# Attention logits of a four-layer graph network: products and gates kept in PSUM, a signed scalar product

## The chip, the cores and the metric

The kernel runs on one core of one Trainium2 chip. The metric is the device time of one execution in microseconds (us), from the first to the last instruction with what lies around them. All data are float32. The engines are TensorE (PE; its weight loads are shown as PEld), VectorE (DVE), ScalarE (ACT), GpSimd (POOL) and SyncE (SP, which only issues DMAs here).

## The reference, cut to what matters

The network has four message-passing layers over one graph of 3,125 nodes and 103,125 edges. The change touches only layer 1, a graph attention whose edge features are 64 scalars `s` and 32 vectors `v` of three components. For each edge, with `y0` and `y1` (three numbers) its spherical harmonics:

```python
def _cg_tp(s, v, y0, y1, w_ss, w_sv, w_vs, w_vv0, w_vv1):
    out_s = concatenate([w_ss * s * y0, w_vv0 * (einsum('eci,ei->ec', v, y1) / SQRT3)])
    out_v = concatenate([(w_sv * s)[:, :, None] * y1, w_vs[..., None] * v * y0,
                         w_vv1[..., None] * (cross(v, y1) / SQRT2)], axis=1)
    return out_s, out_v
msg_s = (s_n @ Ws_src)[src] + (s_n @ Ws_dst)[dst]        # and msg_v in the same way
w1 = rbf @ W_rbf                                         # 224 weights per edge
m1_s, m1_v = _cg_tp(msg_s, msg_v, y0, y1, *split(w1))
a = (m1_s @ W_alpha).reshape(e, H, AS_)
a = sum(where(a > 0, a, 0.2 * a) * alpha_dot, axis=-1)   # the logits
val_s, val_v = m1_s @ Ws_val, einsum('ecx,cd->edx', m1_v, Wv_val)
val_v = val_v * sigmoid(val_s @ Wg)[..., None]
val_s = sigmoid(val_s)
m2_s, m2_v = _cg_tp(val_s, val_v, y0, y1, w2_ss, w2_sv, w2_vs, w2_vv0, w2_vv1)
h = (m2_s @ Ws_vlin, einsum('ecx,cd->edx', m2_v, Wv_vlin))
```

## The kernel before, in words

`attention_logits` (L967) makes the logits and the rows `h` for all edges. The edges are taken in 202 groups of 512: each partition holds 4 edges (`TPG`), and most tiles have the shape 128 x 4 x something. Every engine runs its own program, a loop over groups `g` unrolled four times (`rounds`), and the engines meet by counting semaphores. `hold(eng, k, sem, value)` is one wait and one increment of an idle counter; the order of instructions on each engine is the order in which they are written.

In step `g` each engine does parts of several groups:

- DVE: `head(g+1)`, `mid(g)`, `tail(g-1)`. The head adds the two gathered rows (L1253) and makes the first tensor product in `feat`: scalars by weights (L1259, L1261), all nine products of the three components with the three harmonics in `vy` (`with_planes`, L1237), the scalar product as a reduce (L1263), the cross product as two subtractions (`cross`, L1242 and L1243), and three products with the weights (L1264, L1267, L1269). The mid takes what TensorE made of it: L1278, L1282 and L1287 make the gated vector `vec`, L1279 and L1289 the logits, then `with_planes` again (`ty`, L1237), a reduce (L1296) and `cross` into `z`. The tail (L1304, L1308) finishes the row that is stored. `HEAD`, `MID` and `TAIL` count the instructions of each part, for the waits.
- ACT, one queue in this order (L1093 to L1137): `take_feat` for pieces 0 and 1 of group g+1 (PSUM to SBUF, L1101), the copy of the scalars of `c2` for group g-1 into `hrow` (L1108, signals `hs_ready`), `take_feat` of piece 2, four copies of `vec` scaled by y0 (L1113), four copies of `wps` scaled by y0 into `wy` for group g+2 (L1121), three copies of the turned `z` (L1126), then for group g+1 the sigmoid for the gates, the relu, a copy and a sigmoid (L1129 to L1132), and four scaled copies (L1135).
- PE in step g (L1150 on): the second map of group g-1 into `c2` for rows 0 and 1, the turn (transpose) of `feat` piece 0 of group g+1, second map row 2, turn of piece 1, second map row 3 (this one signals `c2_ready`), turn of piece 2, the weights `wps` of group g+2 (L1189), and then the first map of g+1 (`scal`, `fv`) by rows with the turns of `z` of group g between them. All turns write the one bank `tps`, so each waits until ACT has taken the one before it. The turn of `feat` piece 0 waits for `head_ops`, the turn of `z` piece 0 for all of `mid(g)`, then for `sy_ready` and `vy_ready`.
- POOL issues eight gathers for a group four groups ahead of its head (L1085). SP loads the harmonics, the indices and the radial basis, and stores `hrow`.

PSUM is full: `wps`, `scal` and `c2` have two banks each, `fv` and `tps` one.

## Time and profile before

| | us |
|---|---|
| median of 3 runs (lowest, highest) | 6447.02 (6443.19, 6455.58) |
| the profiled execution: its time | 6445.45 |
| the profiled execution: its span | 6443.7 |
| first L1253 of the logits stage to its last L1108 | 1275.6 to 3695.8 |

Over the whole span PE is busy 75%, DVE 75%, ACT 36% and POOL 66%. In the logits stage the order is different, so the stage is read by itself: by a window over it, by its groups of instructions, and above all by the timeline of one group of edges. A row of a timeline has the start in us from the beginning of the span, the duration, the engine, the line, what it writes and reads, and in brackets how long the engine was idle before it and who released it. Where a helper holds the instruction, the line is that of the helper: both nine-fold products are L1237, both cross products L1242 and L1243, all turns L1144.

### The profile page before, as it was taken

How to read it: one execution, taken by the hardware profiler on the slowest of the kernel's cores; microseconds unless marked ns; L12 is line 12 of the kernel's file. 1: busy time of each engine (PE TensorE's matmuls, PEld its weight loads, DVE VectorE, ACT ScalarE, POOL GpSimd, SP SyncE). 2: the span in 40 equal slices, each digit the busy share in tenths (PEclk: the TensorE clock that was granted, in tenths of full speed). 3: DMA queues.
4: the chain of work that ended last, by engine and by line, in shares of the span. 5: the costliest groups of instructions: out<-in, count | busy, mean ns of one | idle time of the engine just before them, and what ended most of it. 6: DMA issues, size and time to landing. Idle time of an engine off the chain costs nothing. (4 is left out here: it accounts for less than half of the span.)

```text
span 6443.7 us, 162517 instructions
## 1 busy us (share of the span) xinstructions
PE 4855.9 (75%) x45499; PEld 3778.9 (59%) x45500; DVE 4808.7 (75%) x11056; ACT 2316.4 (36%) x6999; POOL 4230.3 (66%) x4250
## 2 busy tenths in 40 slices
PE   6666667488888888888888769877766677777775
PEld 3444445377777777777777757644444464444445
DVE  5777776489989899898998764477777756666665
ACT  1100002266666666666666567400100021000001
POOL 5777775177767777777777347277777727777772
PEclk8888888699999999999999979888888887777777
DMA  3333332133333333333333247222222212222221
GB/s 108 92 92 92 92 92 69 44 94 90 92 89 92 92 89 92 90 91 92 89 92 90 66 148 229 61 73 72 72 72 72 72 38 69 69 69 69 69 69 38
DMA packets 401459, 545.15 MB, mean 85 GB/s; under 512 B 144998, under 2 KB 283382, under 8 KB 401244
## 3 DMA queue, kind: packets, MB, share of 16 engines
q0 software_dynamic: 193920, 331.22, 20.7%
q1 hardware_dynamic: 207452, 212.84, 11.3%
q8 instruction: 46, 0.75, 0.0%
q14 instruction: 41, 0.34, 0.0%
HBM read 464.79 MB, written 78.90 MB: 84 GB/s over the span
## 5 line engine op out<-in xcount | busy, mean ns | idle before, releaser
L816 POOL DMA_INDIRECT e_rows<-tab,e_idx x2424 | 2291.8, 945 | 814.1 <-issue 682.3
L1085 POOL DMA_INDIRECT acc<-tabx,a_idx x1616 | 1682.1, 1041 | 870.4 <-issue 465.2
L861 PE MATMUL e_wps<-e_w,e_hidT 64*128 64x192 f32 (+1 forms) x4848 | 792.9, 461 | 877.1 <-DVE e_hidT L932 874.5
L861 PEld LDWEIGHTS e_wps<-e_w,e_hidT 64*128 64x128 f32 x4848 | 539.7, 250 | 1081.1 <-DVE e_hidT L932 967.8
L846 PE MATMUL e_win<-e_feat,e_ohy 128*32 128x96 f32 (+1 forms) x19392 | 1026.5, 330 | 23.4 <-DVE e_feat L926 21.9
L846 PEld LDWEIGHTS e_win<-e_feat,e_ohy 128*32 128x32 f32 x19392 | 706.6, 131 | 454.2 <-issue 296.5
L917 DVE TENSOR_TENSOR e_feat<-e_wps,e_rows 128x256 f32<-128x256 f32 x606 | 257.3, 425 | 836.7 <-DMA e_rows<-tab,e_idx 758.7
L926 DVE TENSOR_TENSOR e_feat<-e_wps,e_rows 128x384 f32<-128x384 f32 (+1 forms) x1616 | 719.2, 496 | 0.0
L1148 PE MATMUL a_c<-acc,a_buffer 128*128 128x64 f32 (+1 forms) x4848 | 624.7, 272 | 121.8 <-ACT a_buffer L1126 121.8
L835 ACT ACTIVATE e_idx<-src 128x4 int32 (+1 forms) x606 | 123.3, 204 | 1603.1 <-DMA e_rows<-tab,e_idx 1580.1
L1148 PEld LDWEIGHTS a_c<-acc,a_buffer 128*128 128x128 f32 (+1 forms) x4848 | 590.3, 192 | 143.9 <-issue 143.9
L831 ACT ACTIVATE e_tanh<-e_hid 128x512 f32<-128x512 f32 x303 | 181.1, 598 | 1120.6 <-PE e_hid L867 1120.6
L1237 DVE TENSOR_TENSOR acc<-acc 128x1152 f32<-128x1152 f32 x404 | 545.5, 1350 | 0.0
L1101 ACT ACTIVATE acc<-a_tps 128x512 f32<-128x512 f32 (+1 forms) x606 | 361.1, 596 | 390.3 <-PE a_tps L1144 390.3
L1126 ACT ACTIVATE a_buffer<-a_tps 128x512 f32<-128x512 f32 (+1 forms) x606 | 361.2, 596 | 381.2 <-PE a_tps L1144 370.4
L1144 PE MATMUL a_tps<-ident_sb,acc 128*128 128x128 f32 (+1 forms) x2424 | 377.7, 279 | 118.8 <-ACT acc L1101 105.8
L1148 PE MATMUL a_fv<-acc 128*128 128x64 f32 x3232 | 451.7, 262 | 0.0
L1148 PEld LDWEIGHTS a_fv<-acc 128*128 128x128 f32 x3232 | 450.9, 192 | 0.0
L1144 PE MATMUL a_tps<-ident_sb,a_buffer 128*128 128x128 f32 (+1 forms) x2424 | 377.7, 279 | 82.4 <-ACT a_buffer L1126 78.9
L1148 PE MATMUL a_scal<-acc 96*128 96x164 f32 x1616 | 376.8, 314 | 65.2 <-issue 46.9
L920 DVE TENSOR_TENSOR e_ohy<-e_marks,y 128x512 f32<-128x512 f32 x606 | 412.2, 680 | 0.0
L867 PE MATMUL e_hid<-e_ein,e_w 128*128 128x512 f32 (+2 forms) x606 | 360.3, 676 | 19.6 <-DMA e_ein<-in_e64T 7.8
(252 smaller groups left out, 7851.1 us busy)
## 6 DMA issues: line engine op xcount, KB each, us to landing
h_d<-a_buffer SPq DMA_DIRECT2D x202, 322.0 KB, 2.5
s_hin<-h_d SPq DMA_DIRECT2D x202, 322.0 KB
e_rows<-tab,e_idx POOLq DMA_INDIRECT x2424
e_ein<-in_e64T SPq DMA_DIRECT2D x202, 128.0 KB
acc<-tabx,a_idx POOLq DMA_INDIRECT x1616
a_ein<-in_e_h SPq DMA_DIRECT2D x202, 64.0 KB
e_ein<-in_e16T SPq DMA_DIRECT2D x202, 32.0 KB
tab<-p_rows SPq DMA_DIRECT2D x36, 160.0 KB
```

The lines of the kernel that those rows point to most:

```text
L816: pool.indirect_dma_start(out=rows[:, s, t, :], out_offset=None, in_=k.tab0, in_offset=bass.IndirectOffsetOnAxis(ap=idx[:, s, t:t + 1], ax ...
L846: mm = pe.matmul(win[NB * y:NB * (y + 1), s, 0:many * V], ohy[:, s, t, y, :], feat[:, s, t, first:first + (many - 1) * pitch + 1:pitch, :] ...
L861: mm = pe.matmul(wps[:, e, 2 * u + j, 0:WC], hidT[half, edges], w2[half, :], start=True, stop=True)
L867: mm = pe.matmul(hid[:, :], w1[:, :], ein[:, :], start=True, stop=True)
L920: v.tensor_tensor(ohy[:, e, :, :, :], over(oh[:, e, :, :], 2, 4), harmonics(g), ALU.mult)
L926: ins = v.tensor_tensor(f[:, :, slot(field):slot(field) + (many - 1) * pitch + 1:pitch, :], over(w[:, :, wc:wc + V], 2, many), planar(r[:, ...
L1085: pool.indirect_dma_start(out=rows[:, b, q, :], out_offset=None, in_=table, in_offset=bass.IndirectOffsetOnAxis(ap=idx[:, b, end, q:q + 1] ...
L1101: act.activation(featT[0:m, q, :], tps[0:m, :], ACT.Copy).then_inc(f_taken, 1)
L1126: act.activation(zT[0:m, q, :], tps[0:m, :], ACT.Copy).then_inc(z_taken, 1)
L1144: mm = pe.transpose(tps[0:m, q * P:(q + 1) * P], src[:, q, col:col + m], k.ident[:, :])
L1148: return pe.matmul(out, srcT[0:rows, j, q * P:(q + 1) * P], cw[key], start=True, stop=True)
L1237: return v.tensor_tensor(to[:, :, :, :, :].rearrange("p t j x c -> p t j (x c)"), over(of, 2, 3), y[:, :, 0:9].unsqueeze(3).to_broadcast([ ...
```

## The change

- The harmonics come as 13 numbers per edge (y13: 1 3 1 2, 2 2 3 1, 3 | 1 2 3 | 0) where there were 10. The nine products are laid out so that the four products to be subtracted stand four planes behind the four they are subtracted from. One subtraction gives the three components of the cross product and, because ACT first negates one harmonic in `ybuf` (plane 4, new `minus_ready`), two terms of the scalar product; one addition of the ninth plane completes it. The reduce and `cross` go away. In the head that is one subtraction of 128x512 into `dc` and one addition; in the mid two subtractions of 128x256 straight into `z` and one addition. Two weight tables have their rows in the new order.
- ACT copies the nine planes into spare columns of PSUM: into `wps[:, :, 224:233]` with the scaled weights of the head (`wy_ready`), and into `c2[:, :, 192:201]` for the mid, behind the copy into `hrow` (new `yc_ready`, for which `ty` in `mid(g)` waits).
- ACT writes the weights scaled by y0, the gates and the rectified scalars back into the PSUM tiles they were read from. `feat` scalars and the pair of it become one DVE product of 128x512. PE, which writes `scal` again, waits for the fourth operation of the mid where it waited for the third.
- The head has 8 instructions where it had 10; the mid has 9 as before.

```diff
-    HEAD, MID, TAIL = 10, 9, 2
+    HEAD, MID, TAIL = 8, 9, 2
-        ybuf = scratch(U, TPG, 10)
+        ybuf = scratch(U, TPG, 13)
-        wy = scratch(TPG, 96)
-        vy, red, cr = scratch(TPG, 3, 3, V), scratch(TPG, V), scratch(TPG, 3, V)
+        vy, dc = scratch(TPG, 3, 3, V), scratch(TPG, 4, V)
-        gate, rect = scratch(2, TPG, V), scratch(2, TPG, S)
-        w_ready, wy_ready = sem("a_w_ready"), sem("a_wy_ready")
+        w_ready, wy_ready, yc_ready = sem("a_w_ready"), sem("a_wy_ready"), sem("a_yc_ready")
+        minus_ready = sem("a_minus_ready")
...
@@ -1067,7 +1066,7 @@
                         sp.dma_start(ybuf[:, b, :, :].rearrange("p t y -> p (t y)"),
-                                     a["y10_t"][bass.ds(g + 3, 1), :, :].rearrange("o p c -> p (o c)")).then_inc(y_in[b], 16)
+                                     a["y13_t"][bass.ds(g + 3, 1), :, :].rearrange("o p c -> p (o c)")).then_inc(y_in[b], 16)
 
@@ -1106,19 +1105,26 @@
                         act.activation(hrow[:, o, :, 0:S], c2[:, :, 0:S], ACT.Copy).then_inc(hs_ready, 1)
+                    if inside(g, n):
+                        if isinstance(g, int) and g == 1:
+                            hold(act, k, c2_ready, 1)
+                        act.activation(c2[:, :, 192:201], ybuf[:, s, :, 0:9], ACT.Copy).then_inc(yc_ready, 1)
                     take_feat((2,))
...
                         for q in range(TPG):
-                            ins = act.activation(z[:, s % 2, q, 160:352].rearrange("p (x w) -> p x w", x=3)[:, :, 0:V], vec[:, q, :, :],
-                                                 ACT.Copy, scale=ybuf[:, s, q, 9:10])
+                            ins = act.activation(z[:, s % 2, q, 160:352].rearrange("p (x w) -> p x w", x=3)[:, :, V:2 * V], vec[:, q, :, :],
+                                                 ACT.Copy, scale=ybuf[:, s, q, 12:13])
                         ins.then_inc(vy_ready, 1)
...
                         hold(act, k, y_in[b], uses(s, i, 2) * 16 + 16)
+                        act.activation(ybuf[:, b, :, 4], ybuf[:, b, :, 4], ACT.Copy, scale=-1.0).then_inc(minus_ready, 1)
+                        hold(act, k, minus_ready, g + 3)
                         hold(act, k, w_ready, g + 3)
                         for q in range(TPG):
-                            ins = act.activation(wy[:, q, :], wps[:, q, 0:96], ACT.Copy, scale=ybuf[:, b, q, 9:10])
+                            act.activation(wps[:, q, 0:96], wps[:, q, 0:96], ACT.Copy, scale=ybuf[:, b, q, 12:13])
+                        ins = act.activation(wps[:, :, 224:233], ybuf[:, b, :, 0:9], ACT.Copy)
                         ins.then_inc(wy_ready, 1)
@@ -1126,13 +1132,13 @@
                         hold(act, k, c_ready, g + 2)
-                        act.activation(gate[:, o, :, :], scal[:, :, 128:160], ACT.Sigmoid)
-                        act.activation(rect[:, o, :, :], scal[:, :, S:2 * S], ACT.Relu, scale=0.8)
+                        act.activation(scal[:, :, 128:160], scal[:, :, 128:160], ACT.Sigmoid)
+                        act.activation(scal[:, :, S:2 * S], scal[:, :, S:2 * S], ACT.Relu, scale=0.8)
                         act.activation(lk[:, o, :, :, 16], scal[:, :, 160:164], ACT.Copy)
...
                         for q in range(TPG):
-                            ins = act.activation(z[:, o, q, 0:S], z[:, o, q, 96:160], ACT.Copy, scale=ybuf[:, (s + 1) % U, q, 9:10])
+                            ins = act.activation(z[:, o, q, 0:S], z[:, o, q, 96:160], ACT.Copy, scale=ybuf[:, (s + 1) % U, q, 12:13])
                         ins.then_inc(sy_ready, 1)
@@ -1191,7 +1197,7 @@
                         if not isinstance(g, int) or g >= 0:
-                            hold(pe, k, mid_ops, g * MID + 3)
+                            hold(pe, k, mid_ops, g * MID + 4)
                             hold(pe, k, sig_ready, g + 1)
@@ -1224,7 +1230,7 @@
                 alpha = cw["L1_c0"][:, S:2 * S].rearrange("p (q c) -> p q c", q=H)
-                leak = red[0:96, :, 0:16]
+                leak = dc[0:96, :, 0, 0:16]
                 wchain.link(v.tensor_tensor(leak, alpha, adot[0:96, :].rearrange("p (q c) -> p q c", q=H), ALU.mult))
@@ -1235,12 +1241,11 @@
                     return v.tensor_tensor(to[:, :, :, :, :].rearrange("p t j x c -> p t j (x c)"), over(of, 2, 3),
-                                           y[:, :, 0:9].unsqueeze(3).to_broadcast([P, TPG, 9, V]).rearrange("p t (j x) c -> p t j x c", j=3),
+                                           y.unsqueeze(3).to_broadcast([P, TPG, 9, V]).rearrange("p t (j x) c -> p t j x c", j=3),
                                            ALU.mult)
 
-                def cross(to, of, signal):
-                    v.tensor_tensor(to[:, :, 1:3, :], of[:, :, 1, ::-2, :], of[:, :, 2, 0:2, :], ALU.subtract).then_inc(signal, 1)
-                    v.tensor_tensor(to[:, :, 0:1, :], of[:, :, 1, 1:2, :], of[:, :, 2, 2:3, :], ALU.subtract).then_inc(signal, 1)
+                def turned_planes(of):
+                    return of.rearrange("p t j x c -> p t (j x) c")
 
@@ -1256,27 +1261,28 @@
                     hold(v, k, head_ops, at + 1)
-                    v.tensor_tensor(feat[:, :, 0:S], wy[:, :, 0:S], m[:, :, 0:S], ALU.mult).then_inc(head_ops, 1)
-                    with_planes(vy, mv, y).then_inc(head_ops, 1)
-                    v.tensor_tensor(feat[:, :, 96:160], wps[:, :, 96:160], m[:, :, 0:S], ALU.mult).then_inc(head_ops, 1)
+                    v.tensor_tensor(feat[:, :, 0:192].rearrange("p t (o c) -> p t o c", o=2)[:, :, :, 0:S],
+                                    wps[:, :, 0:192].rearrange("p t (o c) -> p t o c", o=2)[:, :, :, 0:S],
+                                    over(m[:, :, 0:S], 2, 2), ALU.mult).then_inc(head_ops, 1)
+                    with_planes(vy, mv, wps[:, :, 224:233]).then_inc(head_ops, 1)
+                    v.tensor_tensor(pair[:, :, :, 0:V], over(wps[:, :, S:96], 2, 3), mv, ALU.mult).then_inc(head_ops, 1)
                     hold(v, k, head_ops, at + 3)
-                    v.tensor_reduce(red[:, :, :], vy[:, :, 0, :, :].rearrange("p t x c -> p t c x"), AX.X, ALU.add).then_inc(head_ops, 1)
-                    v.tensor_tensor(pair[:, :, :, 0:V], over(wy[:, :, S:96], 2, 3), mv, ALU.mult).then_inc(head_ops, 1)
-                    cross(cr, vy, head_ops)
+                    of = turned_planes(vy)
+                    v.tensor_tensor(dc[:, :, :, :], of[:, :, 0:4, :], of[:, :, 4:8, :], ALU.subtract).then_inc(head_ops, 1)
                     hold(v, k, head_ops, at + 5)
-                    v.tensor_tensor(feat[:, :, S:96], wps[:, :, 160:192], red[:, :, :], ALU.mult).then_inc(head_ops, 1)
-                    hold(v, k, head_ops, at + 8)
-                    v.tensor_tensor(pair[:, :, :, V:2 * V], over(wps[:, :, 192:224], 2, 3), cr[:, :, :, :], ALU.mult).then_inc(head_ops, 1)
+                    v.tensor_tensor(pair[:, :, :, V:2 * V], over(wps[:, :, 192:224], 2, 3), dc[:, :, 1:4, :], ALU.mult).then_inc(head_ops, 1)
+                    v.tensor_tensor(dc[:, :, 0, :], dc[:, :, 0, :], of[:, :, 8, :], ALU.add).then_inc(head_ops, 1)
+                    hold(v, k, head_ops, at + 7)
+                    v.tensor_tensor(feat[:, :, S:96], wps[:, :, 160:192], dc[:, :, 0, :], ALU.mult).then_inc(head_ops, 1)
 
...
                     zz = z[:, s % 2, :, :]
-                    pair = zz[:, :, 160:352].rearrange("p t (x w) -> p t x w", x=3)
                     at = g * MID
...
                     hold(v, k, sig_ready, g + 1)
-                    v.tensor_tensor(t[:, :, :, :], over(fv[:, :, 0:V], 2, 3), planes(y, 0), ALU.mult).then_inc(mid_ops, 1)
-                    v.tensor_tensor(lk[:, s % 2, :, :, 0:16], rect[:, s % 2, :, :].rearrange("p t (q c) -> p t q c", q=H),
+                    v.tensor_tensor(t[:, :, :, :], over(fv[:, :, 0:V], 2, 3), planes(y, 9), ALU.mult).then_inc(mid_ops, 1)
+                    v.tensor_tensor(lk[:, s % 2, :, :, 0:16], scal[:, :, S:2 * S].rearrange("p t (q c) -> p t q c", q=H),
                                     over(adot, 1, TPG).rearrange("p t (q c) -> p t q c", q=H), ALU.mult).then_inc(mid_ops, 1)
@@ -1284,24 +1290,30 @@
                         hold(v, k, vy_ready, g)
-                    v.tensor_tensor(vec[:, :, :, :], t[:, :, :, :], over(gate[:, s % 2, :, :], 2, 3), ALU.mult).then_inc(mid_ops, 1)
+                    v.tensor_tensor(vec[:, :, :, :], t[:, :, :, :], over(scal[:, :, 128:160], 2, 3), ALU.mult).then_inc(mid_ops, 1)
                     hold(v, k, mid_ops, at + 3)
...
                     hold(v, k, mid_ops, at + 4)
-                    with_planes(ty, vec, y).then_inc(mid_ops, 1)
+                    hold(v, k, yc_ready, g + 1)
+                    with_planes(ty, vec, c2[:, :, 192:201]).then_inc(mid_ops, 1)
                     hold(v, k, mid_ops, at + 6)
...
                         hold(v, k, z_turned, g * 3 - 3)
-                    v.tensor_reduce(zz[:, :, S:96], ty[:, :, 0, :, :].rearrange("p t x c -> p t c x"), AX.X, ALU.add).then_inc(mid_ops, 1)
-                    cross(pair[:, :, :, V:2 * V], ty, mid_ops)
+                    of = turned_planes(ty)
+                    v.tensor_tensor(zz[:, :, 2 * V:8 * V].rearrange("p t (u w) -> p t u w", u=2)[:, :, :, 0:V], of[:, :, 0:2, :],
+                                    of[:, :, 4:6, :], ALU.subtract).then_inc(mid_ops, 1)
+                    v.tensor_tensor(zz[:, :, 7 * V:11 * V].rearrange("p t (u w) -> p t u w", u=2)[:, :, :, 0:V], of[:, :, 2:4, :],
+                                    of[:, :, 6:8, :], ALU.subtract).then_inc(mid_ops, 1)
+                    hold(v, k, mid_ops, at + 7)
+                    v.tensor_tensor(zz[:, :, S:96], zz[:, :, S:96], of[:, :, 8, :], ALU.add).then_inc(mid_ops, 1)
 
...
                     v.wait_ge(hs_ready, g + 1)
-                    v.tensor_tensor(t5[:, :, :, :], over(c2[:, :, S:96], 2, 3), planes(ybuf[:, s % U, :, :], 0), ALU.mult).then_inc(tail_ops, 1)
+                    v.tensor_tensor(t5[:, :, :, :], over(c2[:, :, S:96], 2, 3), planes(ybuf[:, s % U, :, :], 9), ALU.mult).then_inc(tail_ops, 1)
                     if not isinstance(g, int) or g >= 2:
@@ -1879,7 +1891,7 @@
         "e64T": edge(i["edge_attr_64"]).T, "e16T": edge(i["edge_attr_16"]).T, "e8T": edge(i["edge_attr_8"]).T,
-        "y10_t": edge(i["edge_attr_4"]).reshape(G, TPG, P, 4)[..., [1, 2, 3, 2, 3, 1, 3, 1, 2, 0]].transpose(0, 2, 1, 3).reshape(G, P, TPG * 10),
+        "y13_t": edge(i["edge_attr_4"]).reshape(G, TPG, P, 4)[..., [1, 3, 1, 2, 2, 2, 3, 1, 3, 1, 2, 3, 0]].transpose(0, 2, 1, 3).reshape(G, P, TPG * 13),
         "ends_t": np.stack([edge(src).reshape(G, TPG, P), edge(dst, fill=N).reshape(G, TPG, P)], 1).transpose(0, 3, 1, 2).reshape(G, P, 2 * TPG),
@@ -1959,10 +1971,11 @@
     a["L1_c3_c"] = const((96, 64), [(0, 0, (64, 64), 1), (64, 0, (32, 64), r3)])
+    riap = lambda r, c, m: [(r, c, m[2]), (r + V, c, m[1])]
     for name, m in (("L1_c4", three), ("L1_c4_f", factors), ("L1_c4_c", bent(three))):
-        a[name] = _place((P, 64), [(0, 0, m[0])] + pair(64, 32, m))
+        a[name] = _place((P, 64), [(0, 0, m[0])] + riap(64, 32, m))
     for name, m in (("L1_c5", three), ("L1_c5_f", factors), ("L1_c5_c", bent(three))):
-        a[name] = _place((P, 64), pair(0, 0, m) + pair(64, 32, m))
+        a[name] = _place((P, 64), riap(0, 0, m) + riap(64, 32, m))
     w = np.zeros((P, SLOTS, D), f)
...
         w[16 * q:16 * q + 16, q, 0:S] = g(1, "Wps")[16 * q:16 * q + 16]
```

## Rows read from the trace of the kernel before

**Rows 1.** Window over the stage: PE, PEld, DVE, ACT, POOL busy, clock, DMA share, GB/s
```profile
2400.00:3400.00 1000.00, 846.69 (x6758) 759.78 (x6757) 900.09 (x1774) 667.72 (x1942) 705.06 (x677) 1.00 0.34 91
```

**Rows 2.** Timeline of one group, 2405 to 2419 us: start, duration, engine, line
```profile
2405.53 0.60 PE L1144 MATMUL a_tps<-ident_sb,a_buffer 128*96 128x128 f32 x4
...
2409.25 0.60 ACT L1126 ACTIVATE a_buffer<-a_tps 128x512 f32<-128x512 f32 x1 [0.90 <-PE a_tps L1144]
...
2410.98 0.56 DVE L1278 TENSOR_TENSOR acc<-a_fv,acc 128x384 f32<-128x384 f32 x1
...
2411.75 0.60 PE L1144 MATMUL a_tps<-ident_sb,acc 128*96 128x128 f32 x4
...
2413.07 0.43 DVE L1289 TENSOR_REDUCE keep<-acc 128x272 f32 x1
...
2413.41 1.35 DVE L1237 TENSOR_TENSOR acc<-acc 128x1152 f32<-128x1152 f32 x1
...
2414.59 0.39 ACT L1108 ACTIVATE a_buffer<-a_c 128x256 f32<-128x256 f32 x1
...
2415.09 0.59 DVE L1296 TENSOR_REDUCE a_buffer<-acc 128x128 f32<-128x384 f32 x1 [0.33 <-DVE acc L1237]
...
2415.47 0.60 ACT L1101 ACTIVATE acc<-a_tps 128x512 f32<-128x512 f32 x1 [0.49 <-PE a_tps L1144]
...
2415.93 0.28 DVE L1243 TENSOR_TENSOR a_buffer<-acc 128x128 f32<-128x128 f32 x1
...
2416.61 0.52 PE L1148 MATMUL a_scal<-acc 96*128 96x164 f32 x2 [0.32 <-issue]
...
2416.84 0.56 DVE L1308 TENSOR_TENSOR a_buffer<-a_buffer,a_c 128x384 f32<-128x384 f32 x1 [0.15 <-DVE a_buffer L1304]
...
2417.31 0.82 DVE L1253 TENSOR_TENSOR acc<-acc 128x640 f32<-128x640 f32 x1
2417.36 0.60 PE L1144 MATMUL a_tps<-ident_sb,a_buffer 128*96 128x128 f32 x4
...
2418.09 0.59 ACT L1126 ACTIVATE a_buffer<-a_tps 96x512 f32<-96x512 f32 x1
```

**Rows 3.** Groups by shape, 2400 to 2447.41 us: count | busy us, mean ns | idle
```profile
L1296 DVE TENSOR_REDUCE a_buffer<-acc 128x128 f32<-128x384 f32 x4 | 2.4, 593 | 1.3 <-DVE acc L1237 1.3
L1242 DVE TENSOR_TENSOR acc<-acc 128x256 f32<-128x256 f32 x4 | 1.7, 420 | 0.0
L1261 DVE TENSOR_TENSOR acc<-a_wps,acc 128x256 f32<-128x256 f32 x4 | 1.7, 418 | 0.0
L1121 ACT ACTIVATE acc<-a_wps,acc 128x96 f32<-128x96 f32 x16 | 4.1, 335 | 0.0
L1131 ACT ACTIVATE acc<-a_scal 128x16 f32<-128x16 f32 x4 | 0.8, 203 | 0.0
```

**Rows 4.** A 128x512 product of DVE in the other layers, from the page
```profile
L920 DVE TENSOR_TENSOR e_ohy<-e_marks,y 128x512 f32<-128x512 f32 x606 | 412.2, 680 | 0.0
```

**Rows 5.** Timeline, first group: the head's last instruction releases a turn on PE
```profile
1280.25 0.56 DVE L1269 TENSOR_TENSOR acc<-a_wps,acc 128x384 f32<-128x384 f32 x1
...
1280.95 1.06 PE L1144 MATMUL a_tps<-ident_sb,acc 128*96 128x128 f32 x4 [12.82 <-DVE acc L1269]
```

**Rows 6.** Timeline, last group: the mid's last instruction releases a turn on PE
```profile
3683.46 0.29 DVE L1243 TENSOR_TENSOR a_buffer<-acc 128x128 f32<-128x128 f32 x1
...
3684.19 1.06 PE L1144 MATMUL a_tps<-ident_sb,a_buffer 128*96 128x128 f32 x4 [3.43 <-DVE a_buffer L1243]
```

**Rows 7.** Timeline near the stage's end, around a fall of the clock
```profile
3671.49 0.52 PE L1148 MATMUL a_scal<-acc 96*128 96x164 f32 x2 [1.17 <-DVE a_buffer L1243]
...
3672.24 0.74 PE L1144 MATMUL a_tps<-ident_sb,a_buffer 128*96 128x128 f32 x4
...
3676.86 0.60 ACT L1126 ACTIVATE a_buffer<-a_tps 128x512 f32<-128x512 f32 x1 [1.00 <-PE a_tps L1144]
```

**Rows 8.** Window there: busy times as in rows 1, then the granted clock
```profile
3673.00:3676.00 3.00, 3.00 (x15) 3.00 (x15) 0.00 (x0) 1.19 (x2) 0.00 (x0) 0.50 0.27 110
```

## The prediction

> **What bounds the kernel now.** The change touches one stage, so I read that stage alone. The window over 1000 us of it has DVE busy 900, PE 847, ACT 668, POOL 705, with the clock at 1.00, TensorE's upper level of 2.4 GHz [rows 1]. DVE is the busiest, but the share doesn't say who sets the pace. For that I read the timeline of one group [rows 2].
>
> Start with PE: the turn of z piece 0 starts at 2405.53 and the next one at 2417.36, so a group takes 11.83 us. Between them, PE and ACT hand one bank to and fro: turn, take by ACT, turn. The third take of z ends at 2409.85, the turn of feat piece 0 starts at 2411.75 (6.22 after the turn of z), ACT's last take of feat starts at 2415.47, the first map at 2416.61, the next turn of z at 2417.36. No row of PE there names DVE as what released it. The mid is done at 2416.21 (L1243) and PE uses it at 2417.36, 1.15 later. So the PE-ACT chain is tight at 11.83 by itself, and DVE runs beside it, its own waits being mostly for its own results: 0.33 before L1296, 0.15 before L1308. Work taken from DVE alone buys little; a delay put into either chain is paid 202 times.
>
> The row that decides is L1108, the copy of c2's scalars, at 2414.59. It belongs to the same step as the L1237 (`ty`) that starts at 2413.41: ACT does it between the takes of feat pieces 1 and 2, and the store's tail, later in DVE's program, waits for it. Today `ty` runs 1.2 us before L1108.
>
> **The change, part by part.**
>
> *DVE's busy time.* Gone per group: two products of 128x256 (0.418 each), two reduces (0.593 each, the head's taken as the mid's), two subtractions of 256 (0.420) and two of 128 (0.29) [rows 2, 3]: 3.44 us. Added: two of 128x512 (0.680 each) [rows 4], two of 256 (0.420) and two of 128 (0.29): 2.78. Net 0.66 less per group. Whether an input lies in PSUM or SBUF makes no difference to 0.01 (L1261 reads PSUM, 0.418, L1242 doesn't, 0.420), so the planes in PSUM cost or give nothing in duration.
>
> *DVE's new waits.* Where an instruction needs no result just made, it starts about 0.09 before its forerunner ends (L1289 at 2413.07 lasts 0.43, L1237 starts at 2413.41). Where it needs the one right in front it starts 0.15 after (L1308) [rows 2]. The head gets two such places: the product with the cross weights right behind the one big subtraction, and feat's last product right behind the addition. In the old head, other work stood between. Each costs 0.15 + 0.09 = 0.24 by that row, the nearest, and I take it; lower end nothing, if the wait is hidden, upper end 0.33 + 0.09 = 0.42, the gap before L1296. Two of these and the 0.18 of overlap lost with two instructions fewer are 0.66: DVE's own way through a group gets no shorter. The Trainium skill's page "VectorE: DVE Perf Modes" says, under "Rules for kernel authors" and "The DRAIN you can't avoid", that for chained operations one should minimize their count and that a semaphore costs nothing extra. The two starts above, 0.09 before and 0.15 after an end, speak against that here; by the rule DVE would keep nearly all of the 0.66. In the forecast this changes nothing, since DVE waits anyway; a rival below takes it up.
>
> *ACT.* Six writes change destination from SBUF to PSUM, four of them ahead of the takes of z (L1121, 0.335 each) [rows 3]. No row has ACT writing PSUM. They get no shorter than the shortest activation, the 0.20 of L1131, and I let them get longer by as much: 0.54 either way for the four. I take nothing, since only source and destination bank change. New are three small activations: the negation (128x4), the planes into wps and the planes into c2 (128x36 each), each about the 0.20 of L1131 [rows 3], and a wait of 0.15 for the negation. The negation, its wait and one copy stand before the takes of z and delay ACT there by 0.55, or 0.4 where they overlap their neighbours. Today ACT can take z 2.62 after its last take of feat started (2418.09 - 2415.47), new 3.0 to 3.2. If z's turn stayed where it is, that would cost 0.4 to 0.6; below it moves later by itself, and this is hidden.
>
> *The new wait of `ty` for `yc_ready`.* The planes for the mid are copied behind L1108. Chain from the turn of feat piece 0: L1108 starts 2.84 later (2414.59 - 2411.75), lasts 0.39, the copy ends about 0.10 after it (0.20 at most), DVE starts 0.14 after that (as PE in rows 5: 1280.95 less 1280.81). So `ty` starts 3.47 after the turn of feat piece 0. Today: 1.66. Queued behind `ty` on DVE are the rest of the mid, for which z's turn on PE waits, the tail, and the next head, for which the next turn of feat waits. Both make a loop. All times from the start of `ty`:
>
> - Mid: 1.35 + 0.33 (the gap before L1296) = 1.68 first subtraction, 2.02 second, 2.36 addition, done 2.64.
> - Loop over z: with a turn of z released by the mid, PE needs 0.44 (3684.19 less 3683.75: two more waits stand behind that for the mid) [rows 6]. Turn of z at 3.08. From there to the turn of feat 6.22 as today: 9.30. Then 3.47: 12.77.
> - Loop over the head: from the last small mid operation to L1253 1.38 (2417.31 - 2415.93), so L1253 at 3.74. Head: 0.82 + 0.15, 512-product to the planes 0.60, planes to pair 1.27, pair to subtraction 0.47, subtraction 0.68 + 0.15, product to addition 0.48, addition 0.29 + 0.15, last product 0.29: 5.35. Head done at 9.09, turn of feat possible at 9.23 [rows 5]. That is 0.07 before the other loop wants it. DVE would have `ty` ready at 9.09 - 0.09 + 2.43 (2413.41 - 2410.98) = 11.43, so it stands 1.3 us there.
>
> So the group takes 12.77 us against 11.83: 0.94 more. In ACT's queue the take of z is wanted at 3.08 + 0.73 = 3.81; ACT's last take of feat starts 0.25 after `ty` (2415.47 is 3.72 after the turn of feat), plus 3.2 at most is 3.45: hidden with 0.36 to spare. Only at the upper end of the in-place writes, 0.54 more, would 0.18 come out of it.
>
> *What else moves.* PE's wait for the mid's fourth instead of third operation: that one ends before `ty` starts, 2.4 us and more before the first map (2416.61), nothing. The load of 13 harmonics in place of 10 is issued three groups ahead; POOL's gathers have slack when the group gets longer (705 of 1000 busy, rows 1). The first and last group have no full loop: 200 steps count.
>
> Sum, against the profiled execution: 6445.45 + 200 x 0.94 = 6633. That execution is 1.6 under the median shown, inside the spread of the runs. What a measurement of this kernel can tell from no change is about 0.2%, 13 us.
>
> **Rivals.**
>
> *The clock falls too.* At the stage's end PE was idle 1.17 us before the first map, and a little later the clock was 0.50, the level of 1.2 GHz [rows 7, 8]. There the way from the turn of z to the end of the third take took 5.22 (3677.46 - 3672.24) against 4.32 today [rows 2]. In my schedule PE idles before the turn of z: the first map starts 1.14 after ACT's last take of feat, at 1.39, today's turn would be at 2.14 (2417.36 - 2416.61 = 0.75 on), the new one is at 3.08: up to 0.94 more idle. That is less than 1.17 and more than the 0.32 before the first map of today, at which the clock holds 1.00. If the clock fell in every group, the loop would be 13.67: 6445 + 368 = 6813; in every fourth, 6678. The Trainium skill's page "TensorE: Matmul & The Clock Gate", Part 1, puts it that the default state is throttled and activity releases it, which agrees with rows 7 and 8. Chance 0.15.
>
> *The head's own waits decide.* If the three waits in the head (two new, one as today) cost 0.33 each instead of 0.15, the head is done at 9.63 and the loop is 9.63 + 0.14 + 3.47 = 13.24: +282, 6727. For: the gap before L1296. Against: the 0.15 of L1308. Chance 0.12.
>
> *The other side: DVE is the bound and gets shorter.* For: DVE is 90% busy, the most of all [rows 1], and loses 0.66 us. At full price: 6445 - 202 x 0.66 = 6312. It decides only if the copy of the planes is done before `ty` is otherwise ready, that is if ACT passes L1108 1.8 us earlier relative to DVE than it does today, and if PE and ACT could go faster than 11.83. Against: both, by rows 2. Chance 0.05. The rule of the Trainium skill's page "VectorE: DVE Perf Modes" named above, count over waits, would point this way.
>
> *The wait is taken up.* `ty` waits, but the slack of 1.15 between the mid's end and z's turn pays for all of it, the group stays at 11.83: 6445. Against: `ty` moves by 1.8 relative to the turn of feat and the release on PE needs 0.44. Chance 0.03.
>
> **How the numbers follow.** The forecast has 0.65. Its own bounds: with 0.14 for the 0.44 and 0.26 for the 0.33 (L1296 has that at times) the loop over z is 12.40 and that over the head 12.63, 6605, and with the head's new waits at nothing 12.40 holds, 6559; with 0.2 for the copy and head waits halfway, 13.0, 6680. I give 6575 to 6750, which leaves out most of the clock case's upper part and the two small ones. Faster 0.05, same 0.02, slower 0.93.
>
> **What would show it.** Right: the turn of z about 12.8 us apart; `ty` (nine-fold product of the mid) idle over 1 us before it, released by the small ACT copy behind the one from c2; PE's turn of z released by DVE; DVE's busy share near 78% of the window (10.65 less 0.66, over 12.77); no change outside the stage. The head's subtraction and last product each with a gap of 0.15 around them. Wrong: `ty` without idle before it; a group under 12.2 us; a clock under 1.00 in the window (then the first rival).

## The result and the profile after

| | before | after |
|---|---|---|
| median of 4 runs each, on one chip (lowest, highest) | 6446.41 (6443.19, 6455.58) | 6863.73 (6858.02, 6874.93) |
| ratio, 95% interval | | 1.0647 [1.0629, 1.0665] |
| span of the profiled execution | 6443.7 | 6863.5 |
| mean of a group, L1253 / L1258 start to start, 2000 to 2600 us | 11.84 | 13.88 |

Slower, as forecast, but by 417 us and not by 188; the range ended at 6750. In the profile after, the lines of the stage are moved: both nine-fold products are L1243, the small copy for the mid is L1111, the negation L1122, the weights in place L1126, the planes for the head L1127, all turns L1150, the products of both maps L1154, the head begins at L1258 and the mid ends at L1309.

Windows of the profile after, the columns as in [rows 1]; the first row answers to that group, the others lie around one fall of the clock:

```profile
2400.00:3400.00 1000.00, 849.05 (x5746) 772.33 (x5745) 746.05 (x1365) 597.04 (x1871) 556.20 (x574) 0.85 0.29 77
...
2407.00:2409.00 2.00, 1.43 (x12) 0.97 (x8) 1.67 (x4) 1.79 (x8) 1.39 (x3) 1.00 0.20 48
2409.00:2410.00 1.00, 0.47 (x3) 0.47 (x4) 0.85 (x3) 0.79 (x4) 0.91 (x1) 0.58 0.40 79
2409.10:2409.20 0.10, 0.00 (x0) 0.00 (x0) 0.10 (x1) 0.10 (x2) 0.10 (x1) 0.78 0.00 0
2409.20:2409.53 0.33, 0.00 (x0) 0.03 (x1) 0.33 (x1) 0.33 (x3) 0.33 (x1) 0.50 0.64 124
...
2410.00:2415.00 5.00, 5.00 (x25) 4.99 (x24) 4.62 (x8) 1.19 (x2) 1.89 (x2) 0.50 0.47 135
2415.00:2429.00 14.00, 14.00 (x66) 12.86 (x66) 7.38 (x16) 7.71 (x25) 7.57 (x8) 0.50 0.21 55
2430.00:2450.00 20.00, 16.09 (x130) 14.53 (x129) 15.16 (x30) 12.88 (x39) 9.45 (x10) 1.00 0.23 62
```

The clock is the third number from the right. It was 1.00 in [rows 1]; now its mean is 0.85, and it jumps between 1.00 and 0.50 (2.4 and 1.2 GHz). The two narrow rows show a fall at about 2409.15 us, with PE busy for 0.00 us. PE's busy share is the same 85%, which hides the change: at 0.50 PE is "busy" all the time because its products last longer (a turn of four takes 1.06 for 0.60).

The timeline of the profile after, first at the upper level, then across the fall (2409 to 2429), then one whole group at the upper level again:

```profile
2402.98 0.60 PE L1150 MATMUL a_tps<-ident_sb,acc 128*96 128x128 f32 x4
...
2405.81 0.39 ACT L1107 ACTIVATE a_buffer<-a_c 128x256 f32<-128x256 f32 x1
...
2406.10 0.20 ACT L1111 ACTIVATE a_c<-acc 128x36 f32<-128x36 f32 x1
...
2406.44 1.35 DVE L1243 TENSOR_TENSOR acc<-acc,a_c 128x1152 f32<-128x1152 f32 x1 [1.73 <-ACT a_c L1111]
...
2409.53 1.06 PE L1150 MATMUL a_tps<-ident_sb,a_buffer 128*96 128x128 f32 x4 [0.79 <-DVE a_buffer L1309]
...
2413.64 0.68 DVE L1271 TENSOR_TENSOR acc<-acc 128x512 f32<-128x512 f32 x1
...
2414.47 0.56 DVE L1273 TENSOR_TENSOR acc<-a_wps,acc 128x384 f32<-128x384 f32 x1
...
2415.01 0.60 ACT L1132 ACTIVATE a_buffer<-a_tps 128x512 f32<-128x512 f32 x1 [1.55 <-PE a_tps L1150]
...
2418.74 1.06 PE L1150 MATMUL a_tps<-ident_sb,acc 128*96 128x128 f32 x4
...
2422.79 1.06 PE L1150 MATMUL a_tps<-ident_sb,acc 128*128 128x128 f32 x4
...
2423.75 1.35 DVE L1243 TENSOR_TENSOR acc<-acc,a_c 128x1152 f32<-128x1152 f32 x1 [3.89 <-ACT a_c L1111]
...
2427.03 1.06 PE L1150 MATMUL a_tps<-ident_sb,a_buffer 128*96 128x128 f32 x4
...
2440.72 0.61 PE L1150 MATMUL a_tps<-ident_sb,a_buffer 128*96 128x128 f32 x4 [0.82 <-DVE a_buffer L1309]
...
2444.45 0.60 ACT L1132 ACTIVATE a_buffer<-a_tps 128x512 f32<-128x512 f32 x1 [0.90 <-PE a_tps L1150]
...
2446.95 0.60 PE L1150 MATMUL a_tps<-ident_sb,acc 128*96 128x128 f32 x4
...
2449.91 0.63 PE L1150 MATMUL a_tps<-ident_sb,acc 128*128 128x128 f32 x4 [0.25 <-ACT acc L1100]
...
2453.51 1.04 PE L1150 MATMUL a_tps<-ident_sb,a_buffer 128*96 128x128 f32 x4 [0.79 <-DVE a_buffer L1309]
```

Read it in three steps.

- The loop of the forecast is there. `ty` (first L1243) starts 3.46 after the turn of feat piece 0 (2406.44 - 2402.98), released by the copy L1111 behind L1107, after DVE stood 1.73. The turn of z starts 3.09 after it (2409.53), released by DVE's L1309. From there to the turn of feat 6.23 (2446.95 - 2440.72).
- So a group at the upper level takes 12.79 (2453.51 - 2440.72). Of 42 groups between 2000 and 2600 us 16 took 12.69 to 12.99.
- Before the turn of z PE now stands idle 0.79 to 0.82, and right there the clock falls. It does so each time: between 1290 and 4100 us the granted clock of this trace falls 120 times; 86 falls begin in this stop and the other 34 within 0.39 behind it, though these stops add up to only 146 us. The group from 2409.53 to 2427.03 takes 17.50, which is 4.71 more: the turns of z up to the third take's end 6.08 for 4.33, from there to the turn of feat 3.13 for 1.90, the three turns of feat 4.05 for 2.96, the rest 4.24 for 3.60. Three of the 42 groups took over 17 us, the other 23 took 13.69 to 14.77.

Waits in 2400 to 2460 us of the profile after (total us, times, longest):

```profile
DVE acc L1243 <- ACT a_c L1111: 6.9, 3, 3.9
...
PE a_tps L1150 <- DVE a_buffer L1309: 2.4, 3, 0.8
```

Groups of DVE, ACT and POOL by shape, 2400 to 3400 us after (busy us, mean ns | idle), where [rows 3] and [rows 4] have those of before:

```profile
L1243 DVE TENSOR_TENSOR acc<-acc,a_c 128x1152 f32<-128x1152 f32 x72 | 97.5, 1354 | 117.5 <-ACT a_c L1111 110.5 <-issue 7.0
...
L1271 DVE TENSOR_TENSOR acc<-acc 128x512 f32<-128x512 f32 x72 | 49.0, 680 | 0.0
```
```profile
L1126 ACT ACTIVATE a_wps<-a_wps,acc 128x96 f32<-128x96 f32 x288 | 72.7, 315 | 15.1 <-ACT acc L1122 15.1
...
L1127 ACT ACTIVATE a_wps<-acc 128x36 f32<-128x36 f32 x72 | 16.0, 223 | 0.0
```
```profile
L1084 POOL DMA_INDIRECT acc<-tabx,a_idx x574 | 556.5, 969 | 445.5 <-DVE acc L1276 284.1 <-issue 161.4
```

Outside the stage nothing changed to speak of: the stage is 418 us longer, the rest of the program 2 us.

### The profile page after: what moved, and what is told of

The parts are those of the page before. It is cut to its first block and busy times, and to the rows that moved or that the text cites. A ratio compares the mean times of both kernels' runs of the same rounds, so it can differ in the third digit from the quotient of the medians.

```text
span 6863.5 us, 163522 instructions
## 1 busy us (share of the span) xinstructions
PE 5208.1 (76%) x45499; PEld 4127.4 (60%) x45500; DVE 4756.2 (69%) x10652; ACT 2397.6 (35%) x7605; POOL 4116.4 (60%) x4250
## 5 line engine op out<-in xcount | busy, mean ns | idle before, releaser
L1084 POOL DMA_INDIRECT acc<-tabx,a_idx x1616 | 1566.6, 969 | 1397.7 <-DVE acc L1276 752.3
L1154 PE MATMUL a_c<-acc,a_buffer 128*128 128x64 f32 (+1 forms) x4848 | 664.3, 283 | 94.1 <-ACT a_buffer L1132 88.7
L1154 PEld LDWEIGHTS a_c<-acc,a_buffer 128*128 128x128 f32 (+1 forms) x4848 | 630.8, 203 | 116.9 <-issue 115.3
L1150 PE MATMUL a_tps<-ident_sb,a_buffer 128*128 128x128 f32 (+1 forms) x2424 | 514.5, 352 | 183.1 <-DVE a_buffer L1309 149.5
L1132 ACT ACTIVATE a_buffer<-a_tps 128x512 f32<-128x512 f32 (+1 forms) x606 | 361.1, 596 | 649.7 <-PE a_tps L1150 648.9
L1154 PEld LDWEIGHTS a_fv<-acc 128*128 128x128 f32 x3232 | 579.2, 240 | 0.0
L1154 PE MATMUL a_fv<-acc 128*128 128x64 f32 x3232 | 551.8, 304 | 0.0
L1154 PE MATMUL a_scal<-acc 96*128 96x164 f32 x1616 | 471.2, 381 | 59.2 <-DVE acc L1243 56.5
L1150 PEld LDWEIGHTS a_tps<-ident_sb,a_buffer 128*128 128x128 f32 (+1 forms) x2424 | 368.0, 185 | 227.2 <-issue 222.7
L1243 DVE TENSOR_TENSOR acc<-acc,a_c 128x1152 f32<-128x1152 f32 x202 | 273.5, 1354 | 333.4 <-ACT a_c L1111 310.8
L1150 PE MATMUL a_tps<-ident_sb,acc 128*128 128x128 f32 (+1 forms) x2424 | 399.0, 290 | 110.6 <-ACT acc L1100 97.5
```

Of the source, the lines that this page charges most:

```text
L1084: pool.indirect_dma_start(out=rows[:, b, q, :], out_offset=None, in_=table, in_offset=bass.IndirectOffsetOnAxis(ap=idx[:, b, end, q:q + 1] ...
L1132: act.activation(zT[0:m, q, :], tps[0:m, :], ACT.Copy).then_inc(z_taken, 1)
L1150: mm = pe.transpose(tps[0:m, q * P:(q + 1) * P], src[:, q, col:col + m], k.ident[:, :])
L1154: return pe.matmul(out, srcT[0:rows, j, q * P:(q + 1) * P], cw[key], start=True, stop=True)
L1243: return v.tensor_tensor(to[:, :, :, :, :].rearrange("p t j x c -> p t j (x c)"), over(of, 2, 3), y.unsqueeze(3).to_broadcast([P, TPG, 9, ...
```

## The experiments

My theory after the result: the late wait makes the loop of 12.8 us and, with it, a stop of 0.8 us of PE before the turn of z; the stop brings the clock down, and that is the other half of the loss. The rivals: the clock falls for another reason (the new writes into PSUM, DVE's shorter program), or the wait alone costs all of it.

A first batch of four went to a chip on which the kernel before itself took 9468.11 us with a mean clock of 0.67 to 0.68. There e1 took 9651.81, e2 9632.46, e3 9674.13 and e4 9592.57 (ratios 1.0195, 1.0189, 1.0227 and 1.0130, each to within 0.0036): in the stage their clocks were 0.66 to 0.75, and the intervals don't tell the late wait alone (e1), the wait taken off (e2) and the filler (e3) apart. This settles nothing for chips where the kernel before has its clock at 1.00 in the stage; e1, e2 and e3 were run again on such a chip, word for word the same, as e6, e7 and e8. e4 was not, so nothing here rests on it.

| | what it is | us | ratio to before [95%] | group us | clock |
|---|---|---|---|---|---|
| after | | 6863.73 | 1.0647 [1.0629, 1.0665] | 13.88 | 0.85 |
| e6 | before, and the late wait | 6986.19 | 1.0854 [1.0831, 1.0877] | 14.34 | 0.83 |
| e7 | after, late wait off `ty` | 6519.09 | 1.0119 [1.0102, 1.0136] | 12.21 | 1.00 |
| e8 | after, PE kept at work, 5 turns | 6635.36 | 1.0297 [1.0280, 1.0315] | 12.81 | 1.00 |
| e9 | the same, 2 turns | 6672.14 | 1.0355 [1.0338, 1.0372] | 13.02 | 0.98 |
| e5 | after, planes from SBUF, early sign | 6450.04 | 1.0012 [1.0002, 1.0021] | 11.89 | 1.00 |
| e10 | e5, late waits put last | 6438.90 | 0.9981 [0.9972, 0.9990] | 11.79 | 1.00 |
| e11 | before, late waits put last | 6410.31 | 0.9937 [0.9923, 0.9951] | 11.64 | 1.00 |
| e12 | e10, head's planes in PSUM | 6361.03 | 0.9870 [0.9855, 0.9885] | 11.43 | 1.00 |
| e13 | e11, head's planes in PSUM | 6352.60 | 0.9857 [0.9842, 0.9872] | 11.37 | 1.00 |
| e14 | before, head's planes in PSUM | 6443.14 | 0.9998 [0.9989, 1.0007] | 11.83 | 1.00 |

(Group: mean over 2000 to 2600 us, start to start of the head's first instruction. Clock: of the window 2400 to 3400 us. Each ratio is to runs of the kernel before on the same chip, whose medians lie between 6442 and 6451 us, so kernels of different chips are compared by their ratios.)

**The wait alone (e1, e6).** The kernel before with one small copy and one wait:

```diff
                         act.activation(hrow[:, o, :, 0:S], c2[:, :, 0:S], ACT.Copy).then_inc(hs_ready, 1)
+                    if inside(g, n):
+                        act.activation(c2[:, :, 192:201], ybuf[:, s, :, 0:9], ACT.Copy).then_inc(yc_ready, 1)
...
-                    with_planes(ty, vec, y).then_inc(mid_ops, 1)
+                    hold(v, k, yc_ready, g + 1)
+                    with_planes(ty, vec, c2[:, :, 192:201]).then_inc(mid_ops, 1)
```

> The kernel before, and of the change only this: ScalarE copies the nine harmonic planes into PSUM behind its copy of c2, and the nine-fold product of the mid waits for it. No signed planes, no in-place writes, no negation. Theory (the wait makes a loop of about 12.8 us per group, and the idle time that it gives TensorE makes its clock fall, together 13.9 us per group): the old mid is 0.16 us longer behind the product, so about 13.9 to 14.1 us per group, 6860 to 6910 us, clock near 0.85 in the stage. Rival A (the in-place writes and the three extra activations cost the time, the wait is harmless): 6450 to 6480, clock 1.00. Rival B (the wait makes the loop but the clock fell for another reason, the new forms on VectorE or the writes into PSUM): 6445 + 200 x 1.1 = 6665, clock 1.00.

> The kernel before with only the copy of the planes into PSUM behind the copy of c2's scalars, and the wait of the mid's nine-fold product for it. Theory (the wait makes the loop, the idle time on TensorE that it leaves makes the clock fall): 13.9 to 14.1 us per group, 6860 to 6910, clock near 0.85 in the stage. Rival A (the in-place writes and small activations are the cost): 6445 to 6480. Rival B (loop from the wait, but the clock falls for another reason): 6665, clock 1.00.

Measured 6986.19, 76 us above what was expected: the one wait costs 544 us, more than the whole change. Its turn of z:

```profile
2417.81 0.61 PE L1146 MATMUL a_tps<-ident_sb,a_buffer 128*96 128x128 f32 x4 [0.95 <-DVE a_buffer L1245]
```

PE stands 0.95 here where it stands 0.79 to 0.82 in the kernel after (the old mid has a reduce and two subtractions behind `ty`), and the clock is lower still, 0.83. The wait with its copy is enough; no write of ACT into `scal` or `wps` is needed for the fall. Here too each of the 104 falls between 1290 and 4100 us begins in this stop or within 1.6 behind its end.

**The wait taken off `ty` (e2, e7).** `ty` reads its planes in `ybuf`; the copy stays, and the tail waits for it:

```diff
-                    hold(v, k, yc_ready, g + 1)
-                    with_planes(ty, vec, c2[:, :, 192:201]).then_inc(mid_ops, 1)
+                    with_planes(ty, vec, y[:, :, 0:9]).then_inc(mid_ops, 1)
```

> The changed kernel with the same copies on ScalarE, but the nine-fold product of the mid reads its planes from the harmonics in SBUF and waits for nothing new; the tail waits for the copy instead. Theory: the wait is gone, TensorE and ScalarE set the pace again, now with the negation, its wait and one copy ahead of the first take of z (ScalarE is free 3.11 us after its last take of feat in the trace of the changed kernel, 2.62 before): 11.83 + 0.45 = 12.3 us per group, 6535 (6500 to 6570), clock 1.00. Rival A (ScalarE's extra work and the in-place writes are the cost): 6860, as the changed kernel. Rival C (the clock falls as soon as a group is longer than 12 us): 6650 or more, clock under 0.95.

> The changed kernel with all its copies on ScalarE, but the nine-fold product of the mid reads its planes in SBUF and doesn't wait. Theory: TensorE and ScalarE set the pace, with the negation, its wait and one copy ahead of the first take of z: 12.3 us per group, 6535 (6500 to 6570), clock 1.00. Rival C (any group longer than 12 us lets the clock fall): 6650 or more, clock under 0.95. Rival E (the planes must be copied late, the order and not the wait counts): 6864.

6519.09, 16 us under the 6535 of the expectation: of 417 us, 341 go with this one wait, and the clock is 1.00. The 76 that stay fit ACT's additions ahead of the takes of z:

```profile
2407.59 0.20 ACT L1122 ACTIVATE acc<-acc 128x4 f32<-128x4 f32 x1
...
2407.92 0.60 PE L1150 MATMUL a_tps<-ident_sb,a_buffer 128*96 128x128 f32 x4
...
2407.99 1.01 ACT L1126 ACTIVATE a_wps<-a_wps,acc 128x96 f32<-128x96 f32 x4 [0.21 <-ACT acc L1122]
2408.90 0.22 ACT L1127 ACTIVATE a_wps<-acc 128x36 f32<-128x36 f32 x1
2409.03 0.60 ACT L1132 ACTIVATE a_buffer<-a_tps 96x512 f32<-96x512 f32 x1
...
2409.65 0.69 DVE L1264 TENSOR_TENSOR acc<-a_wps,acc 128x512 f32<-128x512 f32 x1 [0.82 <-ACT a_wps L1127]
2409.77 0.63 PE L1150 MATMUL a_tps<-ident_sb,a_buffer 128*128 128x128 f32 x4 [0.58 <-ACT a_buffer L1132]
```

The first take of z starts 1.11 after the turn (2409.03 - 2407.92) where it was 0.73 [rows 2], and the next turn waits 0.58 for it: 0.38 of a group that is 0.37 longer. The forecast had named just that, 0.4 to 0.6, for the case that z's turn stays where it is. No run takes the additions away one by one: e5 below drops both copies and moves the negation at once.

**PE kept at work in its stop (e3, e8, e9).** Nothing is waited for; PE only makes turns that no one reads, ahead of the wait for the mid (five in e3 and e8, two in e9):

```diff
                             if q == 0:
+                                if inside(g + 1, n):
+                                    for _ in range(5):
+                                        pe.transpose(tps[:, 0:P], k.ident[:, :], k.ident[:, :])
                                 hold(pe, k, mid_ops, (g + 1) * MID)
```

> The changed kernel, with five more transposes of the identity on TensorE (0.75 us at the full clock, into the bank that is free there) just before it waits for the mid, where it stood idle 0.79 us. Nothing else. Theory (the idle time there makes the clock fall): clock 1.00 in the stage, 12.77 to 12.9 us per group, 6633 to 6660. Rival B (the clock falls for another reason): the five transposes only add work at the lower level, 6864 to 6950.

> The changed kernel with five transposes of the identity on TensorE (0.75 us at the full clock) in the 0.79 us in which it waits for the mid. Theory: clock 1.00 in the stage, 12.77 to 12.9 us per group, 6633 to 6660. Rival B (the clock falls for another reason): 6864 to 6950.

> As with five transposes, but two (0.3 us), so that 0.5 us of idle time stay. Theory: between the two, the clock still falls in some groups, 6660 to 6800, clock 0.90 to 0.98 in the stage. If the idle time counts by its sum and not by this one gap: nearer to 6800. If anything under 0.6 us is harmless: as with five.

Five turns, more work for PE, take 3.5 points off the ratio, 226 us, with the late wait untouched: 6635.36, as expected. This is the test that tells the theories apart: the loop stays (12.81 us), the clock alone comes back. The turn of z in e8, and in e9:

```profile
2418.76 0.61 PE L1150 MATMUL a_tps<-ident_sb,a_buffer 128*96 128x128 f32 x4 [0.24 <-issue]
```
```profile
2414.53 0.61 PE L1150 MATMUL a_tps<-ident_sb,a_buffer 128*96 128x128 f32 x4 [0.56 <-DVE a_buffer L1312]
```

6672.14 for e9, near the lower end of what was expected. With 0.56 of idle time left the clock holds most of the time: 36 of 46 groups in e9 took 12.69 to 12.99, ten in two stretches 13.5 to 13.9. Between 1290 and 3890 us its clock falls 25 times, each time within 0.30 behind this shortened stop.

**Without the copies (e4, e5).** e4 took only the mid's copy and its wait away. e5 is the change without both copies of the planes and with the negation moved up, behind the copy into `hrow`:

```diff
-                    if inside(g, n):
-                        act.activation(c2[:, :, 192:201], ybuf[:, s, :, 0:9], ACT.Copy).then_inc(yc_ready, 1)
+                    if inside(g + 2, n):
+                        hold(act, k, y_in[b], uses(s, i, 2) * 16 + 16)
+                        act.activation(ybuf[:, b, :, 4], ybuf[:, b, :, 4], ACT.Copy, scale=-1.0).then_inc(minus_ready, 1)
...
-                        ins = act.activation(wps[:, :, 224:233], ybuf[:, b, :, 0:9], ACT.Copy)
```

> As the kernel without the new wait, but the copy of the planes into c2 is taken out too. Theory: that copy lies in ScalarE's idle time between two takes of feat, so nothing changes against that kernel: 6535, within 15 us of it. Rival A (each small activation is paid in full, 0.1 to 0.2 us per group): 20 to 40 us less than that kernel.

> The changed kernel with both nine-fold products reading their planes from the harmonics in SBUF, so without the two copies and without the new wait, and with the negation moved up in ScalarE's queue, behind the copy of c2's scalars, where ScalarE stood idle. Signed planes, joint scalar product and in-place writes stay. Theory: nothing is left in either chain that was not there before, TensorE and ScalarE hand over every 11.8 us as in the kernel before, VectorE's 0.66 us less work buys nothing: the time before, within 0.5% of it. Rival D (VectorE was the bound all the same): 1 to 2% faster than before. Rival A (in-place writes into PSUM cost time): 1% slower or more.

e5 is back at the time before, 6450.04, and not under it, though DVE's instructions are 0.68 shorter in sum (below). So I looked for what holds PE and ACT. But the trace of e5 shows another bound already (waits in 2400 to 3400 us):

```profile
DVE acc L1255 <- DMA acc<-tabx,a_idx: 29.4, 85, 0.6
```

In each of its 85 groups there the head waits for the gathered rows, which in the kernel before it does in none. GpSimd's gathers take 1.18 each by the mean there, for 1.04 before, and never pause beyond the 0.30 between two: eight of them make 11.88, and a group takes 11.89. So e5 can't tell what DVE's shorter work is worth.

**The order of waits (e10, e11).** Where PE and DVE wait for several semaphores in a row, the one that comes last now stands last, as here before the second map (four such places, two on PE and two on DVE, all changed together):

```diff
-                        hold(pe, k, z_taken, g * 3)
                         if not isinstance(g, int) or g >= 2:
                             hold(pe, k, tail_ops, (g - 1) * TAIL)
                             hold(pe, k, hs_ready, g - 1)
+                        hold(pe, k, z_taken, g * 3)
```

> The kernel with both planes in SBUF and the negation moved up, and besides the order of some waits turned: on TensorE the wait for the last take of z stands behind the two for the tail and the copy (second map), the wait for the last take of feat behind the two for the mid and the sigmoid (first map); on VectorE the wait for the result just made stands last in two places. Theory (TensorE needs 0.1 to 0.15 us for each wait that stands behind the late one, and the hand-over sets the pace): 0.59 before the second map becomes about 0.3, the group 11.83 - 0.3 = 11.5 us, near where VectorE alone stands (11.43 less 0.2): 6375 to 6395. Rival F (VectorE sets the pace by now): under 0.1 us gained, 6425 or more. Rival G (ScalarE's queue ahead of the first take of z holds the pace): 6440.

> The kernel before with the same waits turned and nothing else. Theory: the same gain on TensorE, but VectorE has 0.66 us more to do less its own two waits, and the group ends at 11.5 to 11.6: 6375 to 6400, no more than 15 us from the kernel with signed planes. If VectorE's shorter work is worth something once TensorE's chain is shorter: 20 to 60 us more than that kernel.

The second map in the kernel before, and in e11:

```profile
2410.39 1.52 PE L1148 MATMUL a_c<-acc,a_buffer 96*128 96x64 f32 x12 [0.59 <-ACT a_buffer L1126]
```
```profile
2405.84 1.52 PE L1148 MATMUL a_c<-acc,a_buffer 96*128 96x64 f32 x12 [0.20 <-ACT a_buffer L1126]
...
2407.38 0.39 PEld L1144 LDWEIGHTS a_tps<-ident_sb,acc 128*96 128x96 f32 x4 [0.15 <-issue]
```

After the take, PE waited 0.59, and 0.20 with the two passed waits ahead of the late one. The four places are worth 41 us in e11 (0.20 a group); its 6410.31 is 10 above what was expected. In e10 the same took only 0.3 points off e5, 20 us, where 55 and more were expected, and the shorter DVE program lost to the longer one by 29 us. The gathers told why:

```profile
L1085 POOL DMA_INDIRECT acc<-tabx,a_idx x688 | 792.5, 1152 | 209.7 <-issue 190.2 <-DVE acc L1263 19.5
```
```profile
L1084 POOL DMA_INDIRECT acc<-tabx,a_idx x679 | 794.0, 1169 | 207.0 <-issue 187.5 <-DVE acc L1268 19.5
```

The first is e11, the second e10. POOL has no pause left but the 0.30 that lies before every gather, and a gather takes 1.15 to 1.17 by the mean where it took 1.04 in the kernel before and 0.97 in the kernel after. Eight gathers with their pauses make 11.65 and 11.80, the groups of both (11.64 and 11.79).

**The head's planes in PSUM, on three kernels (e12, e13, e14).** In each, one copy behind the scaled weights and another operand:

```diff
+                        ins = act.activation(wps[:, :, 224:233], ybuf[:, b, :, 0:9], ACT.Copy)
                         ins.then_inc(wy_ready, 1)
...
-                    with_planes(vy, mv, y).then_inc(head_ops, 1)
+                    with_planes(vy, mv, wps[:, :, 224:233]).then_inc(head_ops, 1)
```

> The kernel after without its late copy and late wait, and with the late waits put last, as in the run of 6438.9; here the head alone reads its nine planes from PSUM again, the mid reads them from SBUF. If GpSimd's gathers set the pace there (back to back, 1.169 us each by the mean, eight to a group, with 1.98 and 1.6 beside a nine-fold product whose two inputs lie in SBUF), the head's product stretches them no more: mean about 1.05, a group 11.5 to 11.6 us, 6385 to 6405 us. If the chain of TensorE and ScalarE sets the pace, the gathers get shorter, idle time appears on GpSimd, and the time stays at 6430 to 6450; one more small copy in front of the takes of z could then cost up to 0.2 us a group, 6480.

> The kernel before with the late waits put last (6410.3 by itself), and the head's nine planes read from PSUM. If the gathers set the pace of that kernel, their mean falls from 1.152 to about 1.04 and the group from 11.64 to 11.3 to 11.5 us: 6340 to 6385. If TensorE and ScalarE set it, 6400 to 6425, with idle time on GpSimd. Against the run above: if the change's arithmetic (0.66 us less of VectorE) is worth anything once both loops are free, the run above is the faster; if VectorE's own waits eat it, the two are within 15 us or this one is faster.

> The kernel before with one part alone: ScalarE copies the head's nine planes into PSUM behind its scaled weights (0.2 us more before the takes of z), and the head's nine-fold product reads them there. Theory: the gathers' mean falls from 1.043 us to 0.98, GpSimd has slack anyway (705 of 1000 us busy), so the time is the same, 6440 to 6460 (0 to +20). Rival: the copy in front of the takes of z is fully on the chain of TensorE and ScalarE, +0.2 us a group, 6485. Other rival: GpSimd does hold this kernel at times, then it is faster, 6400 to 6430.

e13's gathers beside its two nine-fold products, the mid's from SBUF and the head's from PSUM:

```profile
2406.10 1.35 DVE L1238 TENSOR_TENSOR acc<-acc 128x1152 f32<-128x1152 f32 x1
2406.24 2.02 POOL L1085 DMA_INDIRECT acc<-tabx,a_idx  x1 [0.30 <-issue]
...
2411.09 1.16 POOL L1085 DMA_INDIRECT acc<-tabx,a_idx  x1 [0.30 <-issue]
2411.35 1.35 DVE L1238 TENSOR_TENSOR acc<-acc,a_wps 128x1152 f32<-128x1152 f32 x1
2412.56 0.94 POOL L1085 DMA_INDIRECT acc<-tabx,a_idx  x1 [0.31 <-issue]
```

A gather that starts with a product of two SBUF operands takes 2.02 here; beside the product with its planes in PSUM it takes 1.16. Over 2400 to 3400 us of e13 the gathers that overlap the first product by more than 0.1 us take 1.80 by the mean (103 of them), those that overlap the second 1.07 (172). The Trainium skill's page "SBUF — State Buffer", under "Who interferes with whom", says that a DVE instruction with two SBUF inputs contends with GpSimd's reads of SBUF and that one with at most one such input, outside the two-port modes, does not: these means agree. By the ratios e12 is 71 us under e10 and e13 52 under e11; e12 came out 24 us lower than expected, e13 as expected. At 1.3 and 1.4% under the kernel before, e13 is the best version found. In e14 the mean falls from 1.04 ([rows 1], 705.06 over 677) to 0.97 and the time does not move: GpSimd had slack there, and the copy ahead of the takes of z cost nothing.

The signed arithmetic of e12 buys nothing against e13: the two lie within 9 us, the longer program ahead. From its first product to its end the head takes 4.36 in e12 (L1262 to L1274) and 4.23 in e13 (L1260 to L1270), with two instructions more. That is not to say that DVE stands outside what sets the pace. In e13 the gathers still run without a pause (eight make 11.38, a group 11.37); in e12 they do pause, and PE's turn of feat starts 0.15 behind the head's last instruction:

```profile
2409.36 0.29 DVE L1274 TENSOR_TENSOR acc<-a_wps,acc 128x128 f32<-128x128 f32 x1
...
2409.80 0.61 PE L1148 MATMUL a_tps<-ident_sb,acc 128*96 128x128 f32 x4
```

What holds e12 at 11.43 was not tested.

## Why the prediction was wrong, step by step

- **The loop of the new wait: right.** `ty` 3.46 after the turn of feat (3.47 forecast), turn of z 3.09 later (3.08), 6.23 to the next turn of feat (6.22), group 12.79 (12.77). Where the clock is kept up by filler, the kernel takes 6635.36 for a forecast of 6633.
- **DVE: right.** The sum of its durations per group fell from 11.94 to 11.26 (1008.7 us over 84.5 groups, 811.1 over 72.05), 0.68 for a forecast 0.66; the 512-element subtraction took 0.680; the head's new gap is 0.15 (2414.47 less 2414.32), so the rival that put 0.33 there is out. The busy time with overlaps counted once fell by 0.30 only: the overlap of neighbours shrank by 0.38, where the forecast had 0.18. And the head got no shorter, as forecast: its durations add up to 0.49 less, its way from the first product to the end is 4.36 for 4.23 (e12 and e13). The Trainium skill's page "VectorE: DVE Perf Modes" ("Rules for kernel authors") says to minimize the count of chained operations and not the semaphores; here eight instructions take the head 0.13 longer than ten, so the measurement goes against the rule. DVE's share of the window is 75% where 78 was forecast, and 81% in e8, where the clock is up.
- **DVE as the bound: rightly priced low.** That rival is refuted by the kernel before itself and by e13. e13 runs the same instructions on DVE as that kernel, at 11.37 a group. In the kernel before, the mid's first instruction starts 0.15 behind ACT's L1132 in every group looked at (118 of them, 2000 to 3400 us), so DVE is the one that waits, if by only about 0.1; here the row that releases L1278 at 2410.98 [rows 2]:

```profile
2410.43 0.40 ACT L1132 ACTIVATE a_buffer<-a_scal 128x256 f32<-128x256 f32 x1
```

- **ACT: right in mechanism.** The writes in place got shorter, 0.315 for 0.335. The additions cost 0.37 a group in e7 and are hidden behind the late wait in the kernel after, as forecast.
- **The step that failed: the clock.** The forecast worked out "up to 0.94 more idle" of PE before the turn of z, set it between 1.17, at which the clock had fallen, and 0.32, at which it held, and then gave the fall 0.15 and left it out of the time. The stop was 0.79 to 0.82, and the clock did fall there, 120 times between 1290 and 4100 us. It costs 226 us, by e8, against 191 for the loop itself: the term that the sum put at nothing is the larger half of the loss. The comparison was also made with the wrong stop: PE in the kernel before stands 0.59 before each second map (the row shown with e11) and keeps its clock, so 0.32 was not the longest one known to be harmless. That would have made the fall look less likely still; the length of one stop is not a measure to decide it by.
- **The rival that came in was priced low.** "If the clock fell in every group, the loop would be 13.67", 6813. It took 0.90 from the one part of the loop that [rows 7] showed at the lower level in part. The low level stretches every part of the PE-ACT loop: 4.71 in the group shown, which spends all of its time there. The mean group is 13.88, above the 13.67 of a fall in every group, though 16 of 42 groups took no longer than one at the upper level.
- **What I had half:** "work taken from DVE alone buys little" held, but the PE-ACT chain was not tight at 11.83 by the work in it. 0.39 of it was PE passing two waits behind the late one (0.59 to 0.20), and with the waits in the other order GpSimd's gathers were the next bound. The forecast gave the gathers slack by their busy share of 70%; that held for a longer group and failed at 11.8, where their mean rose.

Open is what about the stops of a group brings the clock down. A stop before the turn of z of 0.56 seldom did, of 0.79 to 0.95 often, while a stop of 0.59 before the second map stood in nearly all these kernels, those at 1.00 too, and none of the 120 falls of the kernel after begins there. The filler of e8 both shortens the stop and gives PE more work; in no run was the place of a stop moved with its length kept, or PE's work changed with the stop kept.

## What to carry to other kernels

When a wait is put into a loop of TensorE, work out TensorE's new idle time in each group too; if it adds a stop longer than any at which the trace shows the clock to hold (here 0.8 where 0.59 had held), give the fall a large chance and price it over the whole loop, not over the one step where it begins. Before copying a small operand elsewhere to save a port, look at what the copying engine's queue has ahead of it: a copy behind the weights gained some 50 us (e13), one that `ty` had to wait for cost 544 (e6). And put the wait that comes last at the end of a row of waits. When a run comes out at the old time, look in its trace for a new bound before you take it as proof that the work removed was worth nothing: e5 was held by the gathers.

## What the hardware showed that I had not expected

- Filler on TensorE paid: five turns of 128x128 with no reader took 226 us off, with PE's busy time in the window 841 us at clock 1.00 where it was 849 at 0.85.
- GpSimd's gathers take 0.94 to 1.00 us where no nine-fold product overlaps them (kernel before, mean 0.96), and up to 2.14 beside one whose inputs both lie in SBUF (e11, e13); their mean went from 0.97 in the kernel after to 1.18 in e5, enough to set the pace at eight to a group.
- A wait already passed is not free on TensorE when it stands behind the late one: two of them took 0.39 us before the second map (0.59 to 0.20, e11).
- All 120 falls of the clock in the kernel after (1290 to 4100 us) begin in, or within 0.39 us behind, one stop of some 0.8 us in each group.
- ScalarE wrote the scaled weights into the PSUM bank that it read in 0.315 us, against 0.335 into SBUF.
